# A graph-attention kernel on one core: TensorE's loop that picks el takes two columns per turn, by register offsets, instead of sixteen

## What is computed

```python
el = jnp.einsum('nhf,hf->nh', feat_src, attn_l)
er = jnp.einsum('nhf,hf->nh', feat_dst, attn_r)
e = el[src] + er[dst]
e = jnp.where(e >= 0, e, NEG_SLOPE * e)
e_max = jax.ops.segment_max(e, dst, num_segments=N)
exp_e = jnp.exp(e - e_max[dst])
```

## Time and profile before

| | |
|---|---|
| median of 3 runs | 5374.18 us (5372.75 to 5381.17) |
| the profiled execution | 5383.65 us, span 5381.5 us |
| PE busy | 3719.0 us, 69% of the span |
| DVE, ACT, POOL busy | 52%, 39%, 49% |
| the pick on PE (L1570) | 400.4 to 929.9 us |

### The profile page before, as it was taken

How to read it: one execution, slowest core, us unless ns; L and a number is a source line. 1 busy time by engine, 2 the same in 40 slices (tenths; PEclk the granted TensorE clock), 3 DMA queues, 4 the chain that set the end, 5 groups by cost and what they waited for, 6 DMA issues and landing times.

```text
span 5381.5 us, 82588 instructions
## 1 busy us (share of the span) xinstructions
PE 3719.0 (69%) x15674; PEld 2068.6 (38%) x15675; DVE 2792.5 (52%) x4907; ACT 2086.3 (39%) x5120; POOL 2651.4 (49%) x2782
## 2 busy tenths in 40 slices
PE   4430399866676777779767676777797766777764
PEld 3210398345555555654322222222343222222221
DVE  6300298855665666677444444444553444444445
ACT  3100165134444444445334343434443343444444
POOL 2667300055555555543365565656403666565653
PEclk8765699988988888989888888889898888888987
DMA  7610022365555555555555555555514555555557
GB/s 241 139 46 5 20 60 77 128 185 160 167 160 155 156 153 148 160 147 184 171 172 164 162 172 165 168 156 168 149 68 156 168 170 166 162 166 164 172 163 240
DMA packets 327907, 798.07 MB, mean 148 GB/s; under 512 B 85656, under 2 KB 107818, under 8 KB 326921
## 3 DMA queue, kind: packets, MB, share of 16 engines
q0 software_dynamic: 201376, 631.37, 40.7%
q1 hardware_dynamic: 109241, 134.08, 7.8%
q10 hardware_dynamic: 17232, 31.99, 2.0%
HBM read 712.03 MB, written 84.78 MB: 148 GB/s over the span
## 4 chain that ended last, share of the span: by engine, by line
PE 46%; issue 25%; DVE 8%; another core or an unknown queue 7%; DVEq 4%; SPq 4%; ACT 3%; DMA 2%; ACTq 0%; POOL 0%; POOLq 0%
PE mm L1648 13%; PE tr L1648 10%; PE mm L1477 5%; DVE big L862 3%; PE mm L1626 3%; PE mm L1570 3%; PE sm L1626 3%; SPq L1079 3%; PE tr L1570 3%; PE sm L1514 2%; DVE edge L836 2%; PE tr L1626 1%; PE hist_ps L1626 1%; ACT eler_hots L1397 1%
## 5 line engine op out<-in xcount | busy, mean ns | idle before, releaser
L1274 POOL DMA_INDIRECT edge<-h_tab,row_idx x1564 | 1481.9, 948 | 1223.0 <-SPq L1085 543.9
L1648 PE MATMUL mm<-edge,eler_hots 128*128 x1664 | 945.1, 691 | 571.0 <-issue 320.9
L1397 ACT ACTIVATE eler_hots<-eler_hots,ones 128x256 f32<-128x256 f32 x1272 | 639.2, 502 | 1389.4 <-PE mm L1648 521.8
L1648 PE MATMUL tr<-edge,eler_hots 128*128 x1664 | 900.0, 666 | 172.5 <-issue 102.1
L1274 POOL DMA_INDIRECT rows_wmat<-v_tab,row_idx x782 | 740.8, 947 | 558.6 <-SPq L1085 347.5
L862 DVE TENSOR_TENSOR big<-big,mm 128x512 f32 x832 | 571.8, 687 | 724.3 <-PE mm L1648 439.0
L1388 ACT ACTIVATE eler_hots<-iota,ndrel 128x128 f32<-128x128 f32 x2544 | 882.0, 393 | 157.5 <-issue 0.7
L862 DVE TENSOR_TENSOR big<-big,tr 128x512 f32 x832 | 571.8, 687 | 643.7 <-PE tr L1648 255.4
L1648 PEld LDWEIGHTS mm<-edge,eler_hots 128*128 128x128 f32 x1664 | 326.3, 212 | 1140.8 <-issue 1139.9
L1648 PEld LDWEIGHTS tr<-edge,eler_hots 128*128 128x128 f32 x1664 | 347.6, 215 | 690.4 <-issue 689.1
L1626 PE MATMUL mm<-edge,eler_hots 128*128 128x260 f32 x1176 | 419.0, 442 | 257.5 <-ACT eler_hots L1397 154.5
(11 more groups left out here) (242 smaller groups left out, 3531.7 us busy)
## 6 DMA issues: line engine op xcount, KB each, us to landing
h_tab<-rows_wmat SPq DMA_DIRECT2D x98, 256.0 KB, 2.0
edge<-h_tab,row_idx POOLq DMA_INDIRECT x1564
rows_wmat<-low_tab SPq DMA_DIRECT2D x133, 128.0 KB
ht_tab<-rows_wmat SPq DMA_DIRECT2D x49, 256.0 KB
big<-ht_tab ACTq DMA_DIRECT2D x49, 256.0 KB
v_tab<-rows_wmat ACTq DMA_DIRECT2D x49, 256.0 KB
x_tab<-big SPq DMA_DIRECT2D x49, 256.0 KB, 3.0
rows_wmat<-v_tab,row_idx POOLq DMA_INDIRECT x782
```

Source lines behind the costliest of these rows:

```text
L1274: pool.indirect_dma_start(ring[:, 2 * u + i, :], None, tab, bass.IndirectOffsetOnAxis(ap=row_idx[:, b, n:n + 1], axis=0)).then_inc(a["rows ...
L1397: act.activation(onehot[:, s.j % 2, :, :], dist[:, :, :], ACT.Relu, bias=ones[:, 0:1], scale=-1.0).then_inc(a["onehot_set"], 1)
L1648: pe.matmul(sum_ps[bank][:, :], onehot[:, s.j // 2 % 2, s.j % 2, :], edge[:, ds(slot[0][s.j], D)], start=True, stop=True).then_inc(a["step ...
```

## The change

TensorE's part of the pick becomes three nested hardware loops. The outer one has 66 turns, for two groups each; the next goes over the two groups (`par`, which chooses the bank and the one-hot buffer), the inner one over the two halves of a group (`half`). Its body has 2 columns, 24 matmuls, and each matmul takes the place of its weights (`hot_at`) and of its output from registers. Group 132 stands behind the loops as a loop over halves alone. Only two banks are used, mm0 and mm1, which become the halves of one tensor `mm_pair` so that a register can choose between them. `el_summed` is counted up after each half, so twice per group, and the others' waits are doubled; `el_masked` begins at 2, so that TensorE's wait is the same from the first group on. VectorE, ScalarE and SyncE do the same work as before.

```diff
-        src_hot = part(KT * Q * P).bitcast(BF16).rearrange("p (b k n) -> p b k n", b=2, k=KT)
+        src_hots = part(KT * Q * P).bitcast(BF16)
+        src_hot = src_hots.rearrange("p (b k n) -> p b k n", b=2, k=KT)
...
-        mm = [ps("mm0", [P, D]), ps("mm1", [P, D])]
+        mm_pair = ps("mm_pair", [P, 2 * D])
+        mm = [mm_pair[:, 0:D], mm_pair[:, D:2 * D]]
...
                     if s.past(2):
-                        dve.wait_ge(el_summed, g - 1)
+                        dve.wait_ge(el_summed, g * 2 - 2)
...
                     dve.wait_ge(a_hot_set, g + 1)
-                    dve.wait_ge(el_summed, g + 1)
+                    dve.wait_ge(el_summed, g * 2 + 2)
                     dve.tensor_tensor(picked[:, par, :, :, :],
-                                      sum_ps[(s.j - 2) % 4][:, 0:Q * NA * H].rearrange("p (q h a) -> p q h a", q=Q, h=H),
+                                      mm[(s.j - 2) % 2][:, 0:Q * NA * H].rearrange("p (q h a) -> p q h a", q=Q, h=H),
...
-                    dve.wait_ge(el_masked, g + 1)
+                    dve.wait_ge(el_masked, g + 3)
...
+            dve.sem_inc(el_masked, 2)
             pipelined(dve, PCOLS // Q, 4, 3, pick)
...
                 if s.past(2):
-                    act.wait_ge(el_summed, g - 1)
+                    act.wait_ge(el_summed, g * 2 - 2)
...
-            def pick(s):
-                g, par, bank = s.k, s.j % 2, s.j
-                pe.wait_ge(src_hot_set, (g + 1) * (KT - 1))
-                pe.wait_ge(far_set, g + 1)
-                if s.past(4):
-                    pe.wait_ge(el_masked, g - 3)
-                for q in range(Q):
-                    for kt in range(KT):
-                        for part in range(3):
-                            last = pe.matmul(sum_ps[bank][:, q * NA * H:(q + 1) * NA * H],
-                                             src_hot[:, par, kt, q * P:(q + 1) * P], el_parts[:, part, kt, :, :],
-                                             start=(kt == 0 and part == 0), stop=(kt == KT - 1 and part == 2))
-                last.then_inc(el_summed, 1)
-            pipelined(pe, PCOLS // Q, 4, 0, pick)
+            def pick(g, par):
+                with pe.Fori(0, 2) as half:
+                    pe.wait_ge(src_hot_set, g * (KT - 1) + (KT - 1))
+                    pe.wait_ge(far_set, g + 1)
+                    pe.wait_ge(el_masked, g + 1)
+                    for q in range(Q // 2):
+                        for kt in range(KT):
+                            for part in range(3):
+                                hot_at = par * (KT * Q * P) + half * (Q // 2 * P) + (kt * Q + q) * P
+                                last = pe.matmul(mm_pair[:, ds(par * D + half * (Q // 2 * NA * H) + q * NA * H, NA * H)],
+                                                 src_hots[:, ds(hot_at, P)], el_parts[:, part, kt, :, :],
+                                                 start=(kt == 0 and part == 0), stop=(kt == KT - 1 and part == 2))
+                    last.then_inc(el_summed, 1)
+            with pe.Fori(0, PCOLS // Q // 2) as i:
+                with pe.Fori(0, 2) as par:
+                    pick(i * 2 + par, par)
+            if PCOLS // Q % 2:
+                pick(PCOLS // Q - 1, 0)
```

## The result

The changed kernel takes 5710.04 us (median of four runs, 5695.57 to 5723.85), the one before 5377.68 us in the runs beside it. The ratio is 1.0609, 95% interval 1.0579 to 1.0639: slower by 6.1%, some 330 us. The forecast was 5663 us, inside its range of 5550 to 5830; 47 us are missing from it. The profiled execution of the changed kernel took 5723.85 us, its span 5721.7 (before: 5381.5, so +340.2).

What follows compares the result with a forecast made beforehand. PE's sequencer was to replace PE as the pick's limit: 629 + 131 x 4.5 = 1218.5 us in place of 930.0, 288.5 us more, so a median of 5663 us, range 5550 to 5830.

Steps and rivals of the forecast that it cites:

- What bounds: In the pick, 4.5 us of PE's sequencer work per group would lie over PE's 2.20, VectorE's 1.99 and ScalarE's 1.3.
- Busy near half: Sign: in a stretch such as 700 to 900 us PE is busy near half, VectorE and ScalarE both under half.
- The price of a group: Pick loop: halves of 1.96 and 1.81 us, bank loop 0.48, pair loop 0.27; sum 4.5 us, ends 3.6 and 5.7.
- What was said to cost nothing: In the pick, two banks in place of four, extra el_summed increments, shifted el_masked and existing waits add no time.
- The clock: PE might drop to 1.2 GHz, giving 4.2 us of matmuls per group, still under 4.5; nothing of note changes.
- the 4.46 us of issue: Idle time at 917.87 us in the earlier kernel; it may go, but was left in the sum.
- The slow part: Pick until 629 us, beside GpSimd's gathers: every sequencer instruction dear, about 2 groups done in place of 2.4.
- A: Rival: each matmul in the pick works out its own addresses, 9.3 us per group, +917, 6291 us; 6%.
- B: Rival: register work disappears under PE's queue, 2.2 us a group, old time less at most 4.46 us, 5370 us; 4%.
- C: Rival: slow stretch is code supply, a small loop escapes it; +72 (5446) or less 237 us (5137); 4% each.

## Why the prediction was right

**What bounds.** The forecast said that PE's sequencer would take the place of PE as the limit, with PE and VectorE both under it. The window of 1000 to 1200 us shows it: 61, 41 and 27% busy for PE, VectorE and ScalarE. "Busy near half" was low for PE: a group's matmuls fill 2.93 us (121.75 / 1992 x 48) in place of 2.20. A row of 24 that stands alone takes 1.27 us and not 24 x 45.8 ns = 1.10, because the last one's whole 0.21 us is seen; and in the stretches where the clock was at its lower level a row takes 2.01 us (at 1234.95). Neither is on the path, which is the sequencer's: between 640 and 1247 us every pair of groups takes 9.70 or 9.74 us, whichever rows it has.

**The price of a group** was 4.5 us, by 10 address operations of 0.12 us, four others of 0.10, the branches and 0.1 for issue. It is 4.85. By its terms, for the half that is followed by a jump (2.09 us in place of 1.96): the branch 0.27 for 0.26; the address operations with the issue of matmuls 1.32 for 1.30, where there are nine in place of ten, the seven small ones at 0.135, but the first two at 0.20 and 0.17; the four others 0.50 for 0.40, and of that the one at the top has 0.19. So the count was right within one, the plain operations were right, and the term that was mis-sized is the fused operation with several register terms at the top of the body: three per half, 0.56 us in place of 0.34. The rest of the group (the second half, the bank loop, half a pair loop) is 4.85 - 2.09 = 2.76 us in place of 2.56, with the longer operations of a second half in it.

The 131 groups make that 0.35 us into 46 us. The sum with the measured group is 629 + 131 x 4.85 = 1264.4 us for the end of the pick; its last matmul starts at 1265.4. That is nearly all that the forecast missed. That it fits to 1 us is in part luck: the rows begin 3.9 us later than assumed, with 2.5 groups done in place of 2, and a pause near the end (below) adds over 1 us.

**What was said to cost nothing.** Two banks, their waits, the increments: the run with two banks alone shows 1.0005. The clock: it was granted at 0.91 in the changed kernel's fast part and at 0.50 with one column per turn, and both groups' prices come out by the sequencer's operations alone. The er load held back low_tab for 10.64 us at 844.91, and I had said that four groups, now 18 us, cover it. They do: it is issued before group 104, and from 640 to 1247 us no pair of groups takes more than 9.74 us. Behind that there is one wait in the chain of the changed kernel, of 5.08 us, at 1247.99:

```profile
1247.87 0.12 DVE rows_wmat L653
1247.99 5.08 another core or an unknown queue
1253.09 0.37 DVE edge L661
```

Before it VectorE has set the one-hot of the block (L653), behind it come the next group's one-hots (L661). In the code L661 waits for a group's low parts and for a group of matmuls that was done; ScalarE, which works on the same low parts, waits at the same time, for 5.8 us. That points to the load of the low parts, but no run tests it. On PE the group from 1247.20 takes 6.30 us in place of 5.05. The forecast had let the 4.46 us of issue in the earlier trace rows stand in its sum.

**The slow part.** The forecast kept it until 629 us with 2 groups done. The long row starts at 632.87 us, and 2.35 groups were done by 629 (2.44 before). Its reason for 2 groups, 30 register instructions each as dear as the others, was wrong: on PE they keep their usual length in this stretch (above), and only weight loads and matmuls are slow. The four matmuls by which the changed kernel is behind at 629 us are 11 us, and 6.4 of these are there from the start (406.93 in place of 400.48 us). The mistake cost the sum under 2 us.

**The rivals.** A (each matmul works out its own addresses, 9.3 us per group) needed 48 operations a group; there are 18. B (hidden under PE's queue) is not idle talk: with constant addresses the same loop is at 2.34 us. The hiding is real, but the changed kernel has more than twice PE's 2.20 us of sequencer work in a group. C fell with the changed kernel's own small body, which was slow though it had run before, and with the gathers left out. The loop of eight columns took back its jumps without a loss (0.9985). The Trainium skill ("Runtime: NRT & Kernel Launch", Instruction fetch mechanics) prefers unrolled code for the sake of the fetch; I had added nothing for that, and by this run that was right for a body half as long as the old one.

**What stays open.** On the chips with the slow stretch the gathers cause it; why they do so there and not on another chip, no kernel here can settle, nor why PE's weight loads and matmuls are slow beside them in the pick and its register instructions aren't. In later stages, beside other gathers, the register instructions are long too: in the changed kernel 663 of PE's 13648 sequencer instructions (register loads from DRAM left out, which are long on either chip) last over 500 ns, one of them in the pick; in the kernel with written-out bank, on the second chip, 22 of 13186.

## What to carry to other kernels

Add up what the engine's sequencer has to do per block of work (0.10 us per plain register instruction or wait, 0.13 to 0.14 for a small address with three matmuls behind it, 0.17 to 0.20 for one of several registers, 0.27 for a branch that jumps) and lay it beside the engine's own time for the block: where it is more, the sequencer sets the pace. Where it is less, look at the longest way without a matmul too: on PE it was covered by 17 queued matmuls here, and a longer one was seen as a pause. Make the body long enough, or keep inner indices out of registers, until both are met; the loop itself costs nothing then (eight columns per turn, 0.9985). Before you tune such a loop, look whether something beside it makes the issue of its instructions slow, and on which chips.

## What the runs showed of the hardware that was not expected

- PE's sequencer was at most 17 matmuls ahead. In the kernels with constant addresses (before, two banks, eight columns per turn, the loop over halves) exactly 17 are still to start when it reaches the add at the end of a body, each time in the fast part; in the changed kernel it is mostly 3. In the loop over halves 1.09 us without a matmul, against 17 x 45.8 ns = 0.78 us, is the pause that takes a group from 2.20 to 2.34 us.
- Fused register operations differ in length: 46 to 51 ns for most address operations, 79 for one of the small ones in each half, and with both bank and half in registers 142 or 143 and 120 for the first two of a half. With only one of the two in a register the first is at 79, and the operation at the top is at 64 to 73 without the bank and 127 to 133 with it. That fits a length by the number of register terms; no run tests that by itself. It is the only term of the sum that was off by much.
- The same kernel takes 5378 to 5415 us in three sets and 4143 us on the chip of the second. On the latter the gathers run beside PE at its full rate; on the others PE issues one weight load or matmul per 1.4 us while they run, though POOL issues a gather every 1.25 us on either. Without them 318 us of the gap are gone. The rest (5090 to 4143) lies in later stages, for which no experiment was made. In the kernel with 18 gathers, from 3250 to 3500 us, the register operations of L1648 last 37 to 42 ns on the quick chip and up to 729 ns on the other, PE does 413 and 333 matmuls, GpSimd 201 and 153 instructions, and the granted clock is 1.00 and 0.87. Which of these comes first isn't shown.
- A matmul that takes its weights' and its output's address from a register is issued fast enough for PE's full rate: between two address operations three matmuls start 45 ns apart, which is what they take in a full queue (2.20 us / 48).
- PE's clock was granted at 0.91 (200 us means) in the changed kernel, with pauses of 0.8 to 1.7 us between rows of 24 matmuls, and at 0.50 in the kernel with one column per turn, with 0.35 us at most turns between rows of 12, on another chip. No run here tells which of the differences decides.
